# State-space decays: a minimum on VectorE and exponentials on ScalarE in place of a product scan, with all factors made beforehand

## The reference, cut to what matters

```
a = -exp(A_log) * softplus(raw + dt_bias)                # log decay of a step, per token and head
Lmat[i, j] = exp(sum_{k=j+1..i} a[k])   for i >= j, else 0
Y_diag = (C B^T * Lmat) x        # within a chunk
state' = exp(sum a) * state + B^T (exp(sum of the rest of a) * dt * x)
Y_off  = exp(cumsum a) * (C state)
```

## Time and profile before

| | |
|---|---|
| median of 3 runs | 2140.66 us |
| the profiled execution's own time | 2139.38 us |
| its span | 2137.7 us |
| TensorE busy | 1813.6 us (85%) |
| VectorE busy | 1499.4 us (70%) |
| ScalarE busy | 1006.5 us (47%) |
| GpSimd busy | 446.5 us (21%) |
| the 64 scans (L1233) | 146.2 us, mean 2306 ns |
| the 64 multiplications with the scores (L1274) | 77.0 us, mean 1203 ns |

### The profile page before, as it was taken

How to read it: one execution, slowest core, us unless ns; L and a number is a source line. 1 busy time by engine, 2 the same in 40 slices (tenths; PEclk the granted TensorE clock), 3 DMA queues, 4 the chain that set the end, 5 groups by cost and what they waited for, 6 DMA issues and landing times. The chain is left out here.

```text
span 2137.7 us, 33282 instructions
## 1 busy us (share of the span) xinstructions
PE 1813.6 (85%) x10026; PEld 1244.3 (58%) x10026; DVE 1499.4 (70%) x3126; ACT 1006.5 (47%) x2291; POOL 446.5 (21%) x411
## 2 busy tenths in 40 slices
PE   5279898898898879799956496999989999999898
PEld 2246666566567568699952144565646565555555
DVE  5678788888887852122226596888888888888885
ACT  2132241341341312122112153888888888888886
POOL 2122314314314332422111101001020202020101
PEclk9588899999998989999987697999999999999999
DMA  4501221221122129555525395225243434353311
GB/s 172 169 30 60 79 78 59 69 88 59 59 85 72 57 90 324 184 184 174 174 67 176 102 281 175 66 77 93 70 100 80 90 85 102 80 100 79 80 31 30
DMA packets 143788, 226.09 MB, mean 106 GB/s; under 512 B 17725, under 2 KB 110015, under 8 KB 143648
## 3 DMA queue, kind: packets, MB, share of 16 engines
q1 hardware_dynamic: 124464, 179.95, 27.7%
q0 software_dynamic: 19184, 44.45, 8.2%
HBM read 174.26 MB, written 50.99 MB: 105 GB/s over the span
## 5 line engine op out<-in xcount | busy, mean ns | idle before, releaser
L2243 DVE TENSOR_SCALAR att_scores<-att_psS 128x512 f32<-128x512 f32 x512 | 348.8, 682 | 102.5 <-PE att_psS L2075 86.2
L2192 ACT ACTIVATE att_prob<-att_scores,att_shift 128x512 f32<-128x512 f32 x512 | 383.2, 749 | 30.5 <-DVE att_shift L2259 30.5
L2201 ACT COPY att_pT<-att_psT 128x512 f32<-128x512 f32 x512 | 306.0, 599 | 132.6 <-PE att_psT L2083 130.8
L2251 DVE CUSTOM_DVE_ANT_0 att_scores<-att_scores,first_decay 128x512 f32<-128x512 f32 x512 | 347.6, 679 | 0.0
L2083 PEld LDWEIGHTS att_psT<-ident,att_prob 128*128 128x128 f32 x2048 | 245.2, 142 | 158.8 <-issue 99.8
L2083 PE MATMUL att_psT<-ident,att_prob 128*128 128x128 f32 x2048 | 315.2, 277 | 15.2 <-ACT att_pT L2201 13.7
L2075 PE MATMUL att_psS<-first_ks,first_qs 128*128 128x512 bf16 x512 | 197.6, 387 | 27.7 <-DVE att_scores L2243 23.1
L2097 PE MATMUL att_psO<-att_pT,att_v 128*32 128x512 f32 x1024 | 138.5, 615 | 37.7 <-ACT att_pT L2201 37.7
L1524 DVE TENSOR_SCALAR ffn_hT<-ffn_psH,ffn_b 128x128 f32<-128x128 f32 x156 | 44.2, 344 | 165.6 <-PE ffn_psH L1460 148.8
L1460 PE MATMUL ffn_psH<-ffn_xT,ffn_w 128*128 128x128 f32 x1248 | 150.0, 280 | 11.0 <-issue 10.5
L1460 PEld LDWEIGHTS ffn_psH<-ffn_xT,ffn_w 128*128 128x128 f32 x1248 | 149.4, 197 | 13.7 <-issue 11.9
(11 more groups left out here) (282 smaller groups left out, 2919.0 us busy)
## 6 DMA issues: line engine op xcount, KB each, us to landing
ffn_w<-in_w SPq DMA_DIRECT2D x39, 1024.0 KB
mamba_am<-a_rows SPq DMA_DIRECT2D x64, 512.0 KB, 3.6
first_qs<-q_parts SPq DMA_DIRECT2D x256, 64.0 KB
first_ks<-k_parts SPq DMA_DIRECT2D x256, 64.0 KB
xn<-xn_all SPq DMA_DIRECT2D x16, 512.0 KB, 5.7
ffn_w<-in_w POOLq DMA_DIRECT2D x8, 1024.0 KB, 6.0
att_w<-in_inter POOLq DMA_DIRECT2D x7, 1024.0 KB, 5.5
att_w<-in_outer POOLq DMA_DIRECT2D x7, 1024.0 KB
```

The costliest lines, as they stand in the source:

```text
L2192: nc.scalar.activation(prob[:, n % NP], scores[:, n % NCL], ACT.Exp, bias=shift[:, h % 2, t:t + 1], accum_out=total[:, octet % 2, t, j, i: ...
L2201: nc.scalar.copy(pT[:, h % HEADS_T, :, t * P:(t + 1) * P], bank_of("turn", n)[:].rearrange("p (k q) -> p k q", k=CPB)).then_inc(pT_ready, 1)
L2243: vec.tensor_scalar(scores[:, n % NCL], psS[n % NS][:], -CLAMP, CLAMP, ALU.max, ALU.min).then_inc(clipped, 1)
L2251: vec.tensor_tensor_reduce(scores[:, n % NCL], scores[:, n % NCL], decay[:, FAR - t * P:FAR - t * P + SEQ], 1.0, -2.0 * CLAMP, ALU.mult, A ...
```

## The change

The decay tile is no longer a running product. `time_steps` stores the cumulative sums of the log decays along a chunk (TensorE multiplies with the strict triangles instead of transposing), and keeps, for all 32 chunks at once, everything that was made per batch: the step times decay, both factors of the states, and `minus`, the negated inclusive sum per token. The tile is then exp(min(sum[t], most[s]) - most[s]) with most = -minus: VectorE takes the minimum (`bound`), so that no exponent is positive, and ScalarE takes the exponential head by head in place, with `minus` as its bias. Since the minimum leaves ones outside the triangle, the score tile is multiplied by the triangle (`masked`) once a chunk. One more decay tile is buffered (4 instead of 3), so tiles are made three ahead, four at a batch's start. The output projection of chunks 0 and 1 moves one tile later, behind `diagonal(4)` and `diagonal(6)`.

In `time_steps` (cut: three more pairs of products follow the first, with `tri[d]` into `psF[1]`, `C.ones` into `psF[2]` and `incl[:, d]` into `psM`; ScalarE takes the exponentials of the three `psF`, and VectorE multiplies the first of them with `dt`):

```diff
-                for q in range(NT // PER):
-                    mm = nc.tensor.transpose(psA[:, q], a[:, q * PER:(q + 1) * PER, :]..., C.ident[:])
+                for d in range(2):
+                    for g in range(2):
+                        mm = nc.tensor.matmul(psA[:, d * 2 + g], flat_heads(a[:, d, g * HALF:(g + 1) * HALF]), tri[d], start=True, stop=True)
                 mm.then_inc(a_turned, 1)
+                for d in range(2):
+                    mm = nc.tensor.matmul(psF[0][:, d], tri[1 - d], flat_heads(a[:, d]), start=True, stop=True)
+                mm.then_inc(summed, 1)
...
-                nc.scalar.activation(aT[:, :, 1:P - 1], psA[:, :, 1:P - 1], ACT.Exp).then_inc(aT_ready, 1)
+                nc.scalar.copy(aT[:], psA[:]).then_inc(aT_ready, 1)
...
+                dve.wait_ge(summed, 4)
+                v.tensor_copy(steps.minus[:]..., psM[:]...).then_inc(minus_ready, 1)
```

In `mamba`, TensorE, ScalarE and GpSimd (ScalarE's calls of `decays` stand behind the evictions of `Bl` and `xl`):

```diff
-                    pe.wait_ge(ab_ready, i + 1)
-                    for q in range(3):
-                        for d in range(2):
...
-                            mm = nc.tensor.matmul(sums[:, at:at + CPB * NH], lhs[:], ab[:, d], start=True, stop=True)
-                    mm.then_inc(sums_ready, 1)
-                    pe.wait_ge(fac_ready, i + 1)
+                    pe.wait_ge(fd_ready, i)
                         if u in (4, 6):
                             turn_tile(u // 2 - 2)
+                        elif u in (5, 7):
                             output(u // 2 - 2)
+                def decays(i, u):
+                    t, d = u // 2, u % 2
+                    act.wait_ge(bounded, i * U + u + 1)
+                    for h in range(NH):
+                        ex = nc.scalar.activation(L[:, u % NL, h], L[:, u % NL, h], ACT.Exp, bias=minus[:, d, t, h:h + 1])
+                    ex.then_inc(decayed, 1)
-                    act.wait_ge(sums_ready, i + 1)
-                    nc.scalar.activation(fac[:]..., sums, ACT.Exp).then_inc(fac_ready, 1)
+                    nc.scalar.copy(minus[:], steps.minus[:, :, bass.ds(i * CPB, CPB), :]).then_inc(minus_ready, 1)
...
-                    for t in range(CPB - 1):
-                        squares(i, t)
-                        turned_tile(i, t)
+                    for u in range(NL):
+                        decays(i, u)
+                    decays(i, 4)
+                    squares(i, 0)
+                    decays(i, 5)
+                    turned_tile(i, 0)
+                    decays(i, 6)
+                    squares(i, 1)
+                    decays(i, 7)
+                    turned_tile(i, 1)
+                    squares(i, 2)
+                    turned_tile(i, 2)
-                    pool.wait_ge(dtdec_ready, i + 1)
+                    pool.wait_ge(steps_ready, i + 1)
```

In `mamba`, VectorE (`steps_of` now makes five small operations that take this batch's part of the tables: `dtb`, `most`, `dtdec` and the two of `fac`):

```diff
                 def steps_of(i):
...
-                        v.tensor_tensor_scan(L[:, u % NL]..., am[:, u % NA, at:at + NH * P][:, ::back],
-                                             begin[:, d]..., 0.0, ALU.mult, ALU.add).then_inc(decayed, 1)
+                        v.tensor_tensor(L[:, u % NL], am[:, u % NA].rearrange("p (h t) -> p h t", h=NH),
+                                        most[:, d, t].unsqueeze(2).to_broadcast([P, NH, P]), ALU.min).then_inc(bounded, 1)
-                    v.tensor_tensor(dtdec[:], dtb[:], fac[:, 1], ALU.mult).then_inc(dtdec_ready, 1)
                     def decays(u):
                         t, d = u // 2, u % 2
-                        dve.wait_ge(g_ready, i * CPB + t + 1)
+                        if d == 0:
+                            dve.wait_ge(g_ready, i * CPB + t + 1)
+                            dve.wait_ge(L_ready, i * U + (2 * t - 2 if t >= 2 else 0))
+                            v.tensor_tensor(masked[:, t % 2], gT[t % 2], C.triangles[:], ALU.mult).then_inc(g_masked, 1)
+                            dve.wait_ge(g_masked, i * CPB + t + 1)
                         dve.wait_ge(decayed, i * U + u + 1)
-                        v.tensor_tensor(L[:, u % NL], L[:, u % NL], gT[t % 2][:, d]..., ALU.mult).then_inc(L_ready, 1)
+                        v.tensor_tensor(L[:, u % NL], L[:, u % NL], masked[:, t % 2, d]..., ALU.mult).then_inc(L_ready, 1)
-                        if u >= 5 and u % 2 == 1:
-                            outputs((u - 5) // 2)
+                        if u >= 6 and u % 2 == 0:
+                            outputs((u - 6) // 2)
```

## The result

The changed kernel takes **2159.68 us** (median of 4 runs, 2156.29 to 2161.74) against 2140.93 (2139.45 to 2144.73) for the kernel before on the same chip: ratio 1.0083, 95% interval 1.0064 to 1.0102. It is slower by 0.8%; forecast were 2123 and a gain, with 2150 as the upper end. The profiled execution took 2156.29 itself, its span 2154.5 against 2137.7, and the mean granted clock of TensorE fell from 0.929 to 0.918.

A forecast was written before the change was run, and what follows sets the result against it. VectorE was taken as the loop's fuller engine with TensorE close behind, and a chain as the opening's bound. 8 x (2.5 + 0.3) = 22.4 us gained less 5.5 lost gave 16.9, so 2123 us; 8-in-10 range 2094 to 2150.

The forecast's parts named there:

- Which engine bounds the loop: Tile loop: VectorE is fuller (31.0 of 34.0 us), but TensorE (29.0) limits what relieving VectorE by 5.3 us can gain.
- The loop, 0.3 us gained a batch: Tile loop: 2.2 us gained through TensorE's shorter waits, less 1.9 for collisions, leaves 0.3 (-0.6 to +2.2).
- the collisions: Tile loop: GpSimd and VectorE operations with two SBUF operands block each other; two hits on the chain, 2 x 0.95 us.
- The wait of 1.99 falls to 1.4: TensorE's wait before chunk 1's first product: minimum and mask take 1.6 us in place of 2.2.
- The moved output product, 0.7 us of new wait twice: TensorE before chunks 2 and 3: output product no longer covers VectorE's work on `psY`; 2.4 us against 1.7.
- The opening, 2.5 us gained a batch: Each batch's opening: 2.2 us from the shorter chain, less 0.5 for the multiplication of tile 1, plus 0.8 from the clock.
- The time steps, 5.5 us once: Time-step stage: added products and eight sums lose 7.2 us at half clock, 3 at full clock; 5.5 taken.
- The lock decides: slower: Rival, tile operations reading SBUF twice: 0.95 us whenever GpSimd is in front; four more hits give 2153 us; chance 0.18.
- VectorE as the bound: Rival, tile loop: VectorE bounds it and TensorE's waits fold in, 57 us gained, 2082 us; chance 0.11.

The follow-up runs named there:

- a_both_psum: Changed kernel with the masked scores and the minimum's bound read from PSUM, so no tile operation has two SBUF operands: 2123.8 us, 0.9914 of the kernel before.
- b_factors: Kernel before, scan and masks kept, with the factors of states and far part made for all batches in the time steps: 2113.7 us, ratio 0.9872.
- a_fill: Changed kernel plus idle TensorE products, four before the third state product and five before chunk 1: 2118.3 us, 0.9877 of the kernel before.
- a_fill_states: Changed kernel plus only the four idle TensorE products before the third state product, none before chunk 1: 2141.6 us, 1.0007 of the kernel before.

## Why the prediction was wrong

- *Which engine bounds the loop.* Right: at full clock VectorE is busy 3.4 us less of 31.9, and the loop is 0.22 us shorter. With the lock gone it is busy 5.7 us less (26.17; 5.3 was forecast), and the loop of 33.25 only 1.6 us shorter: TensorE's waits set it.
- *The loop, 0.3 us gained a batch.* Near at full clock (34.90 to 34.68), but only because two misses nearly cancel: without collisions the loop is 1.6 us shorter where 2.2 were forecast, and the collisions take back 1.4 where 1.9 were. **This term holds the step that failed**: it was worked out from the one loop of the earlier trace rows, with clock 1.00, as if all were like it. Three of the seven loops of before were at 0.83 to 0.88 and 2.8 to 4.7 us longer, in a trace that was at hand: 12.0 us above 7 x 34.90. After, the seven are 31.5 above 7 x 34.68. This term, +19.5 us over seven loops, stands nowhere in the sum, which counted the clock in the opening only. In the trace it is more than the whole of the 16.8 us by which the kernel became slower.
- *The wait of 1.99 falls to 1.4.* Wrong: 2.74. The minimum and the mask alone would nearly have done it (1.60 in `a_both_psum`), but two collisions came on the chain of `y`. The count of two per loop was about right; their place, in TensorE's longest wait, was not looked for.
- *The moved output product, 0.7 us of new wait twice.* Right in place: waits before chunks 2 and 3 come, and those for tiles and for `yT` go. Wrong in size: at full clock the new waits are 1.56 and 0.94, 2.5 in place of 1.4 (2.2 without the lock), so the move, which was to gain 0.1 against the 1.54 for `yT`, costs 1.0. What it does to the clock was missing.
- *The opening, 2.5 us gained a batch.* Measured 7.2 over seven, 1.0 each. The chain was read rightly: where the loop is left alone, it gains 19.0 over seven, 2.7 each. Here the longer waits for `xdd` (2.31 by the lock, which had been allowed 0.5 in all) and a clock of 0.87 to 0.91, where six openings of `b_factors` have 0.93, take back most.
- *The time steps, 5.5 us once.* The stage took from its first load to the mixer's first 19.87 us before and 93.38 - 70.47 = 22.91 after: 3.0, what the prediction gave for full clock from the start. The clock rose midway, as supposed (0.50 from 84 to 88 us, 0.95 from 88 to 94), and the eight sums took 4.2 us where 8.1 had been counted.
- *The rivals.* "The lock decides: slower" named the right mechanism, at 0.18, and priced it by its stalls at 2153. Its price ran over the clock: with the stalls kept and the clock held (`a_fill`) the kernel is faster than before. VectorE as the bound is refuted by `a_both_psum`, where it is busy 26.2 us of a loop of 33.25. The range ended at 2150, since no case in it had the loop at half clock.

The Trainium skill (TensorE: Matmul & The Clock Gate, A second HAM failure mode: psum-queue depth-cycling) describes a kernel in which small idle gaps between groups of products make the clock swing between its two levels, at a cost paid between the bursts. The runs agree: waits of 0.75 to 2.74 us, and loops between 34.7 and 41.4. It speaks against this change, and belonged among the rivals.

**Open** is what exactly tips the clock. A wait of 1.99 us before chunk 1 goes with full clock in all seven loops of `b_factors` and with 0.83 in some of the kernel before; 2.74 goes with 1.00 once; and after a wait of 1.60 `a_both_psum` still has loops at 0.91. What TensorE did ahead of the wait counts too (`a_fill_states`), but what of it does, no run here separates. So these runs explain why this kernel became slower, but give no rule by which the number of slow loops could have been forecast.

## What to carry to other kernels

Cut every batch of the loop at the same instruction and read the granted clock of each before working out a change from one of them; a loop's time at full clock and how often it has full clock are two terms. A change that takes work off another engine but lengthens one wait of TensorE by under a microsecond can cost several (here 1.99 to 2.74 us, and loops 3.7 to 6.7 us longer than at full clock), and the cheapest test is a few idle products in that wait. If an operation of VectorE gets a second SBUF operand while GpSimd works beside it, put one operand into PSUM.

## What the runs showed of the hardware

- A wait of 2.7 us was followed by 13 us at 0.50 of the clock, in which TensorE was busy throughout; in one loop of seven the same wait was followed by full clock. Nine idle products a batch removed 41 us from the kernel after and 18 from the kernel before.
- The lock shows on both tile operations, with two SBUF operands each: `L1277` and `L1315` take up to 2.07 us (alone 1.21), GpSimd's `xfd` 2.02 in the median where it took 1.04 in the kernel before. With one operand of each in PSUM, the maximum of 64 is 1.22.
- The table load at 396.27 starts 0.02 us behind the end of the eviction and the exponential 0.01 behind its own end: no drain on either side. Exponentials of 128x128 follow 0.30 us apart (32 in 9.46); 0.26 had been estimated.
